# Second stage of a fused attention and mixture-of-experts kernel: norm rows by ScalarE, routing weights from one exponential, slot bases in the rank product, three mixture banks

## The chip, the cores and the metric

One core of a Trainium2 chip runs the whole program. The metric is the device time of one execution in microseconds (us). Three runs of the kernel before gave 1202.75, 1204.52 and 1208.31 us, so the median is 1204.52 us. Engines are named as in the profile: PE is TensorE, DVE is VectorE, ACT is ScalarE, POOL is GpSimd, and SP issues most of the DMAs. PEld is PE's weight load.

## The reference

`x` is 32 samples of 112 rows by 256, and `ctx` is 32 samples of 375 rows by 256. Four residual layers follow one another:

```python
x = x + xattn0(ctx, layernorm(x))         # 16 heads; queries from x, keys and values from ctx
x = x + ffn0(layernorm(x))                # 8 experts relu(x W_e + b_e), mixed by the counts of all top-2 choices
x = x + xattn1(layernorm(x), ctx, ctx, mask)   # softmax(q k^T / 16 + mask * -1e9) v
x = x + ffn1(layernorm(x))                # 8 experts of 256-512-256, each token goes to its top 2

# ffn1
w, idx = top_k(xt @ Wg.T + bg, 2)
w = softmax(w, axis=1)
comb = (one_hot(idx, 8) * w[..., None]).sum(axis=1)
out = einsum('eto,te->to', y, comb)
```

The layer norm divides `x - mean` by `sqrt(var + 1e-5)`. The weight of each of the two experts of a token in `ffn1` is a softmax over its two largest logits.

## The kernel before

The program has three stages. The first does `xattn0` and counts the choices of `ffn0`. It leaves `x_res` (the rows after `xattn0`) and `xT_hi`, `xT_lo` (their norm rows, transposed, as two float16 parts). The third stage runs the experts of `ffn1` over rows that were sorted by expert in DRAM (`dispatch`). The change is in the second stage, `middle_phase`, which spans 585 to 949 us of the profile. Its order of work is written out by hand and unrolled. It has 39 steps. Step `u` does five things on five samples, each where it exists:

- `f`, steps 0 to 31: `ffn0`'s mixture for groups of four samples (`GT` = 448 rows). A step does four mixtures, `mix(0)` to `mix(3)`. In each, PE multiplies six 128x128 by 128x448 float16 products into a PSUM bank (L1035), and DVE adds the clipped result to `acc` (L1199 for the first expert, L1203 for the others). Mixture `k` writes bank `k % 2`, so PE waits before it until DVE has read the mixture two places back (`acc_rdy`).
- `a`, sample `u-4`: PE transposes `acc` back into bank 2 (L1051) and DVE adds it to `x_res` (L1231). DVE takes mean and variance (L1212, L1215). POOL makes `rstd` of the variance (L965, L967). DVE makes the norm rows `x2n` (L1245). PE transposes them (L1075), ACT copies them out (`x2nT`, L1159), and PE makes the scores with `ctxT` in bank 4 (L1095). ACT and POOL also split a piece of `ffn1`'s weights into float16 parts (`w_hi` L1155, `w_lo` L994).
- `o`, sample `u-5`: DVE adds the mask and takes the row maximum (L1223), ACT takes the exponential (L1134), PE transposes it into bank 5 (L1061), ACT copies it out (`probsT`, L1139), PE multiplies with `ctx_rows` (L1069), and DVE adds the result to the residual, which gives `x3` (L1291; the profile calls this tile `we`, whose memory it uses).
- `r`, sample `u-6`: DVE takes the statistics of `x3` (L1212, L1215 again), POOL makes `rstd` and `ln_shift` = -mean * rstd (L981), ACT writes the norm rows into `rows` (L1149), PE transposes them (L1082), ACT and DVE make `xT_hi` and `xT_lo` of them (L1163, L1298), and PE makes the routing logits in bank 7 (L1106).
- `k`, sample `u-7`: DVE adds the bias to the logits, finds the two largest and their places, and makes the one-hot rows `first` and `second` and their sum `chosen` (L1250 to L1267). The softmax of two numbers is made of `gap` = second minus largest logit: ACT takes its exponential (L1142), and DVE makes `gap_sum`, `unscaled` and `first_w` (L1274, L1281, L1284). PE ranks the tokens of each expert in bank 3 (L1088 within the sample, L1089 by the running counts `cum`). DVE adds the expert's first slot (`slot_base`), picks the two slots of each token and rounds them to integers (`slots_at`, L1306 to L1314). POOL scatters `rows` to the two slots with two indirect DMAs (L1011).

Each engine works its own list in order, and semaphores join the lists. POOL's list is of importance here. In a step it stands: the two scatters of the step before, `rstd` of `a` (L965, L967), `rstd` and `ln_shift` of `r`, `mask_add` (L987), `w_lo` (L994), the token numbers (L1001), then the scatters of this step, which wait for `slots_at`.

Of the kernel before, what the change touches and what calls it, by code (L numbers as in the profile page):

```python
# [742 lines left out]
def middle_phase(nc, ctx, dram, keep):  # L743
# [143 lines left out]
    with nc.Block() as block:  # L887

        @block.sync
        def _(sp):  # L890
# [60 lines left out]
        def _(pool):  # L951
# [17 lines left out]
            def step(t, u, on):  # L969
                f, a, o, r, k = on  # L970
                if a:
                    rstd("ag2", "eps2", "rs2", 0, cnt(t, u - LAG_ATT, 1, 1))
                if r:
# [45 lines left out]
        def _(pe):  # L1019
            pe.wait_ge(m["consts"], 3)  # L1020

            nc.tensor.matmul(psum[:, 0, 0:E], ones[:], gate_counts[:], start=True, stop=True).then_inc(m["share_ps"], 1)
            pe.wait_ge(m["share_rdy"], 1)

            def mixture(t, u, k):
# [5 lines left out]
                wait(pe, m["acc_rdy"], cnt(t, u, 4, k - 1))  # L1031
                n = 0
                for w, x in ((we_hi, xT_hi), (we_hi, xT_lo), (we_lo, xT_hi)):
                    for kc in range(DC):
# [4 lines left out]

            def step(t, u, on):  # L1040
# [43 lines left out]
                if k:  # L1084
# [609 lines left out]
```

## Time and profile before

| | us |
|---|---|
| median of three runs | 1204.52 |
| the profiled execution | 1202.87 |
| its span in the profile | 1201.1 |
| PE busy (share of the span) | 998.3 (83%) |
| DVE busy | 812.5 (68%) |
| ACT busy | 533.8 (44%) |
| POOL busy | 437.8 (36%) |

The table is a sum over three stages with different limits. What matters for the change is a stretch of the second stage in which all five parts run, 646.70 to 892.79 us, and the four steps behind it, which have no mixtures. "Idle before, releaser" in a row is how long the engine stood idle before that instruction and what it then had waited for. Of the engine PE the rows show the granted clock as a share of 2.4 GHz. Matmuls are pipelined, so rows of a group overlap, and the starts of rows tell more than their ends.

### The profile page before, as it was taken

The numbers are of one execution on the slowest core, as the hardware profiler recorded it, in microseconds if no ns is written. First come the engines' busy times: TensorE is split into PE (matmuls) and PEld (weight loads), VectorE is DVE, ScalarE is ACT, GpSimd is POOL, SyncE is SP. The second block draws the span as 40 slices with busy tenths as digits, with TensorE's granted clock in tenths as the row PEclk, the third lists the DMA queues.
The fourth block names the chain that finished last, engine by engine and source line by source line (L and its number), as shares of the span: only waits on it lengthen the run. The fifth ranks groups of instructions, "written<-read, shape, count | busy, mean of one in ns | idle before, by whom it ended". The sixth has DMA issues, their size and how long they took to land. (4 is left out here: it accounts for less than half of the span.)

```text
span 1201.1 us, 30730 instructions
## 1 busy us (share of the span) xinstructions
PE 998.3 (83%) x10536; PEld 706.0 (59%) x10536; DVE 812.5 (68%) x2319; ACT 533.8 (44%) x1055; POOL 437.8 (36%) x616
## 2 busy tenths in 40 slices
PE   3688889888888988876499999999986289999993
PEld 2366666666666666654255555555554168888872
DVE  4567777777777777764468888888887436666652
ACT  1365666565566666544113232233333045555551
POOL 4322222222222222200115555555556335555444
PEclk9999999999999999988599999999998579999997
DMA  4543333333333343210445555555554135555443
GB/s 126 148 123 117 105 114 112 110 107 114 118 104 117 101 120 105 86 38 2 128 133 166 151 150 150 152 153 150 151 156 133 50 106 89 101 92 94 86 63 36
DMA packets 104712, 133.93 MB, mean 112 GB/s; under 512 B 23806, under 2 KB 93902, under 8 KB 104398
## 3 DMA queue, kind: packets, MB, share of 16 engines
q1 hardware_dynamic: 91024, 113.86, 32.5%
q0 software_dynamic: 13536, 18.10, 8.8%
q8 instruction: 88, 1.44, 0.5%
q14 instruction: 64, 0.52, 0.2%
HBM read 93.78 MB, written 38.68 MB: 110 GB/s over the span
## 5 line engine op out<-in xcount | busy, mean ns | idle before, releaser
L612 DVE TENSOR_REDUCE smax<-psum 112x2 f32<-112x750 f32 x256 | 235.9, 933 | 120.6 <-PE psum L355 120.6
L526 ACT ACTIVATE probsT<-psum 125x896 f32<-125x896 f32 x192 | 175.9, 916 | 39.2 <-PE psum L370 39.2
L1454 POOL DMA_INDIRECT out_dram<-y,token_at x70 | 109.9, 1570 | 117.1 <-DMA out_dram<-y,token_at 61.0
L1535 ACT ACTIVATE h<-psum,b 128x256 f32<-128x256 f32 x140 | 58.8, 471 | 102.5 <-PE psum L1482 102.5
L296 POOL TENSOR_TENSOR ctx_lo<-ctxT,ctx_hi 128x750 f16<-128x750 f32 x32 | 51.7, 1614 | 133.1 <-ACT ctx_hi L533 133.1
L1011 POOL DMA_INDIRECT dispatch_dram<-rows,slots_at x64 | 64.0, 1000 | 94.1 <-DVE slots_at L1314 78.3
L1035 PE MATMUL psum<-xT_hi,we_hi 128*128 128x448 f16 x256 | 71.2, 360 | 26.2 <-DVE acc L1203 12.8
L390 PE MATMUL psum<-probsT,v_aug 125*32 125x112 f32 x3072 | 90.2, 267 | 0.0
L355 PE MATMUL psum<-k_stack,q_stack 63*128 63x375 f16 x512 | 84.9, 329 | 2.1 <-ACT xnT L566 1.3
L1203 DVE SCALAR_TENSOR_TENSOR acc<-psum,neg_bias,acc 128x448 f32<-128x448 f32 x112 | 75.7, 677 | 8.6 <-PE psum L1035 8.6
L370 PE MATMUL psum<-q_stack,k_stack 64*128 64x112 f16 x1536 | 70.3, 210 | 8.2 <-ACT probsT L526 6.8
L390 PEld LDWEIGHTS psum<-probsT,v_aug 125*32 125x32 f32 x3072 | 74.1, 112 | 5.0
L288 POOL TENSOR_SCALAR ln_var<-ln_mv 112x1 f32<-112x1 f32 x32 | 7.1, 222 | 190.2 <-DVE ln_mv L624 190.2
L1035 PE MATMUL psum<-xT_hi,we_lo 128*128 128x448 f16 x256 | 71.0, 360 | 0.0
L1035 PE MATMUL psum<-xT_lo,we_hi 128*128 128x448 f16 x256 | 70.6, 358 | 0.0
L370 PEld LDWEIGHTS psum<-q_stack,k_stack 64*128 64x128 f16 x1536 | 50.9, 95 | 33.5 <-ACT probsT L526 19.2
L1482 PE MATMUL psum<-x_hi,w_hi 128*128 128x256 f16 x280 | 56.1, 281 | 9.7 <-DVE x_lo L1549 5.8
L1134 ACT ACTIVATE probs<-probs,exp_bias 112x375 f32<-112x375 f32 x32 | 19.4, 607 | 100.0 <-DVE exp_bias L1226 100.0
L1482 PE MATMUL psum<-x_hi,w_lo 128*128 128x256 f16 x280 | 55.2, 280 | 0.0
L1482 PE MATMUL psum<-x_lo,w_hi 128*128 128x256 f16 x280 | 55.0, 279 | 0.0
L1549 DVE TENSOR_TENSOR x_lo<-psum,x_hi 128x512 f16<-128x512 f32 x35 | 24.1, 689 | 43.3 <-ACT x_hi L1526 43.3
L1069 PE MATMUL psum<-ctx_rows,probsT 125*112 125x256 f32 x192 | 49.8, 397 | 2.9 <-issue 2.9
(215 smaller groups left out, 2405.1 us busy)
## 6 DMA issues: line engine op xcount, KB each, us to landing
ctxT<-in_ctxT_dram SPq DMA_DIRECT2D x64, 375.0 KB, 4.2
k_stack<-k_hi_dram SPq DMA_DIRECT2D x64, 188.0 KB, 2.7
ctx_rows<-in_ctx_dram SPq DMA_DIRECT2D x32, 375.0 KB
rows_e<-dispatch_dram SPq DMA_DIRECT2D x70, 136.0 KB, 2.5
w_raw<-in_w_dram SPq DMA_DIRECT2D x32, 256.0 KB, 4.6
k_hi_dram<-k_hi SPq DMA_DIRECT2D x32, 188.0 KB, 1.9
k_lo_dram<-k_lo SPq DMA_DIRECT2D x32, 188.0 KB, 1.9
k_stack<-k_lo_dram SPq DMA_DIRECT2D x32, 188.0 KB, 2.8
```

Source lines behind the costliest of these rows:

```text
L296: nc.gpsimd.tensor_tensor(ctx_lo[:, u % 2, :, :], ctxT[:, u % 2, :, :], ctx_hi[:, u % 2, :, :], ALU.subtract).then_inc(m["ctxlo_ready"], 1)
L355: last = nc.tensor.matmul(psum[:, pair_bank(s) + a, 0:KV], queries(rows, b4, s, 128), keys_at(rows, b4, s, 0, KV), start=True, stop=True)
L370: last = nc.tensor.matmul(psum[:, a, r * S:(r + 1) * S], keys_at(rows, b4, 4 * hg + r, c * KC, 128), queries(rows, b4, 4 * hg + r, S), sta ...
L390: last = nc.tensor.matmul(bank_d[32 * j:32 * j + 32, g * S:(g + 1) * S], v_aug[:, b4d, cc, h, :], probsT[:, b2d, cc, h // 8, h % 2, h // 2 ...
L526: nc.scalar.activation(probsT[:, p, c, hg, :, :, :].rearrange("p k h q -> p k (h q)"), psum[0:KC, 0:2, 0:4 * S], ACT.Exp, scale=float(HD) ...
L612: nc.vector.reduce_max(smax[:, (u - LAG_B) % 2, 2 * (s % 4) + s // 4::PAIRS], psum[0:S, pair_bank(s):pair_bank(s) + 2, 0:KV], AX.X).then_i ...
L1011: nc.gpsimd.indirect_dma_start(dram["dispatch"], bass.IndirectOffsetOnAxis(slots_at[:, uk % ROW_SLOTS, n:n + 1], 0), rows[:, uk % ROW_SLOT ...
L1035: last = nc.tensor.matmul(psum[:, k % 2, 0:GT], w[:, kc, e, hc * 128:(hc + 1) * 128], x[:, kc, bass.ds(g0, GT)], start=(n == 0), stop=(n = ...
L1203: nc.vector.scalar_tensor_tensor(out, psum[:, k % 2, 0:GT], neg_bias[:, hc, e:e + 1], out, ALU.max, ALU.add).then_inc(m["acc_rdy"], 1)
L1454: nc.gpsimd.indirect_dma_start(dram["out"], bass.IndirectOffsetOnAxis(token_at[:, n % 2, s:s + 1], 0), y[:, n % 2, s, :], None, compute_op ...
L1482: last = nc.tensor.matmul(psum[:, 1 + c // 2, (c % 2) * TILE:(c % 2 + 1) * TILE], w[:, bass.ds(e, 1), kc, c * 128:(c + 1) * 128].rearrange ...
L1535: nc.scalar.activation(h[:, c, :], psum[:, 1 + c // 2, (c % 2) * TILE:(c % 2 + 1) * TILE], ACT.Relu, bias=b1[:, c, bass.ds(e, 1)]).then_in ...
```

## The change

It has five parts, all in the second stage.

1. `x2n` moves from DVE to ACT. POOL makes a second `ln_shift` (`shift2`), right behind `rstd` of `a`, and ACT computes `x * rstd + shift` behind `probsT`.
2. The routing weights come from `exp(logits - largest)` of all eight logits, by one ACT instruction. One DVE instruction multiplies them with `chosen` and sums them (`weight_sum`), and its reciprocal is `first_w`. `gap`, `gap_sum` and the `unscaled` of before go.
3. The slot bases are a 113th row of `cum` (and `ones` gets a 113th row), so the second rank product adds them. `slot_of` goes.
4. Two DVE instructions that multiply and sum pick the two slots straight from PSUM, in place of two products and a reduction.
5. The rank product moves from bank 3 to bank 5, behind the transposed exponentials, with two waits for it on PE. Mixtures take banks 0, 1 and 3 in turn, and PE waits for the mixture three places back.

```diff
 # POOL, first in a step
                 if a:
-                    rstd("ag2", "eps2", "rs2", 0, cnt(t, u - LAG_ATT, 1, 1))
+                    v = cnt(t, u - LAG_ATT, 1, 1)
+                    rstd("ag2", "eps2", "rs2", 0, v)
+                    wait(pool, m["rs2"], v)
+                    wait(pool, m["x2n_rdy"], cnt(t, u - LAG_ATT - 1, 1, 1))
+                    apart(pool)
+                    nc.gpsimd.tensor_scalar(ln_shift[:, 0, :], ln_mv[:, 0, 0:1], ln_rstd[:, 0, :], -1.0, ALU.mult, ALU.mult).then_inc(m["shift2"], 1)
...
 # PE
+        return MIX_BANKS[(4 * (t * TURN + u) + k) % len(MIX_BANKS)]      # (0, 1, 3)
-                wait(pe, m["acc_rdy"], cnt(t, u, 4, k - 1))
+                wait(pe, m["acc_rdy"], cnt(t, u, 4, k + 1 - len(MIX_BANKS)))
-                        last = nc.tensor.matmul(psum[:, k % 2, 0:GT], ...
+                        last = nc.tensor.matmul(psum[:, mix_bank(t, u, k), 0:GT], ...
...
                     wait(pe, m["exp_rdy"], cnt(t, uo, 1, 1))
                     wait(pe, m["pT_rdy"], cnt(t, uo - 1, 1, 1))
+                    wait(pe, m["pick_rdy"], cnt(t, uk - 1, 2, 2))
...
                     wait(pe, m["chosen_rdy"], cnt(t, uk, 1, 1))
                     wait(pe, m["cum_rdy"], cnt(t, uk - 1, 1, 1))
-                    nc.tensor.matmul(psum[0:S, 3, 0:E], before[:], chosen[:], start=True, stop=False)
-                    nc.tensor.matmul(psum[0:S, 3, 0:E], ones[:, 0:S], cum[:], start=False, stop=True).then_inc(m["rank_done"], 1)
+                    if o:
+                        wait(pe, m["pT_rdy"], cnt(t, uo, 1, 1))
+                    if isinstance(t, int) and t * TURN + uk == 0:
+                        pe.wait_ge(m["weights_in"], 16 * N_W)
+                    rank = psum[0:S, RANK_BANK, RANK_AT:RANK_AT + E]
+                    nc.tensor.matmul(rank, before[:], chosen[:], start=True, stop=False)
+                    nc.tensor.matmul(rank, ones[:, 0:S], cum[:], start=False, stop=True).then_inc(m["rank_done"], 1)
...
 # ACT
+                if a:
+                    xrow = x_res[:, bass.ds(t * TURN + ua, 1), :].rearrange("p o d -> p (o d)")
+                    wait(act, m["shift2"], cnt(t, ua, 1, 1))
+                    apart(act)
+                    wait(act, m["x2nT_done"], cnt(t, ua - 1, 1, 1))
+                    nc.scalar.activation(x2n[:], xrow, ACT.Identity, bias=ln_shift[:, 0, :], scale=ln_rstd[:, 0, :]).then_inc(m["x2n_rdy"], 1)
                 if k:
-                    wait(act, m["gap_rdy"], cnt(t, uk, 1, 1))
-                    nc.scalar.activation(gap_exp[:], gap[:], ACT.Exp).then_inc(m["gexp_rdy"], 1)
+                    wait(act, m["negtop_rdy"], cnt(t, uk, 1, 1))
+                    wait(act, m["pair_rdy"], cnt(t, uk - 1, 1, 1))
+                    nc.scalar.activation(logit_exp[:], logits[:], ACT.Exp, bias=neg_top[:]).then_inc(m["lexp_rdy"], 1)
...
 # DVE
-                if a:
-                    v = cnt(t, ua, 1, 1)
-                    wait(dve, m["rs2"], v)
-                    wait(dve, m["x2nT_done"], cnt(t, ua - 1, 1, 1))
-                    nc.vector.tensor_scalar(x2n[:], xrow(ua), ln_mv[:, 0, 0:1], ln_rstd[:, 0, :], ALU.subtract, ALU.mult).then_inc(m["x2n_rdy"], 1)
...
-                    nc.vector.tensor_tensor(gap[:], top8[:, 1:2], top8[:, 0:1], ALU.subtract).then_inc(m["gap_rdy"], 1)
+                    nc.vector.tensor_scalar(neg_top[:], top8[:, 0:1], -1.0, None, ALU.mult).then_inc(m["negtop_rdy"], 1)
...
-                    wait(dve, m["gexp_rdy"], v)
-                    nc.vector.tensor_scalar(gap_sum[:], gap_exp[:], 1.0, None, ALU.add).then_inc(m["pair_rdy"], 1)
+                    wait(dve, m["lexp_rdy"], v)
+                    wait(dve, m["chosen_rdy"], v)
+                    nc.vector.tensor_tensor_reduce(out=unscaled[:], in0=logit_exp[:], in1=chosen[:], scale=1.0, scalar=0.0,
+                                                   op0=ALU.mult, op1=ALU.add, accum_out=weight_sum[:]).then_inc(m["pair_rdy"], 1)
...
-                    nc.vector.scalar_tensor_tensor(unscaled[:], second[:], gap_exp[:], first[:], ALU.mult, ALU.add).then_inc(m["pair_rdy"], 1)
...
-                    nc.vector.tensor_tensor(slot_of[:], psum[0:S, 3, 0:E], slot_base[:], ALU.add).then_inc(m["pos_rdy"], 1)
-                    nc.vector.tensor_tensor(cum[:], cum[:], chosen[:], ALU.add).then_inc(m["cum_rdy"], 1)
-                    wait(dve, m["pos_rdy"], v)
-                    nc.vector.tensor_tensor(picked[:, 0, :], slot_of[:], first[:], ALU.mult).then_inc(m["pick_rdy"], 1)
-                    nc.vector.tensor_tensor(picked[:, 1, :], slot_of[:], second[:], ALU.mult).then_inc(m["pick_rdy"], 1)
-                    wait(dve, m["pick_rdy"], cnt(t, uk, 3, 2))
-                    nc.vector.tensor_reduce(slots[:], picked[:], AX.X, ALU.add).then_inc(m["pick_rdy"], 1)
+                    for n, which in enumerate((first, second)):
+                        nc.vector.tensor_tensor_reduce(out=picked[:, n, :], in0=psum[0:S, RANK_BANK, RANK_AT:RANK_AT + E], in1=which[:], scale=1.0,
+                                                       scalar=0.0, op0=ALU.mult, op1=ALU.add, accum_out=slots[:, n:n + 1]).then_inc(m["pick_rdy"], 1)
+                    nc.vector.tensor_tensor(cum[0:S, :], cum[0:S, :], chosen[:], ALU.add).then_inc(m["cum_rdy"], 1)
```

The instructions of DVE in the middle of a full step, before, from the statistics of `x3` to the second mixture:

```order
L1212 BN_STATS ln_stats<-we 112x6 [waits m_x3_rdy]
L1215 BN_AGGR ln_mv<-ln_stats 112x2 [waits m_st3]
L1245 TENSOR_SCALAR x2n<-x_res,ln_mv,ln_rstd 112x256 [waits m_x2nT_done,m_rs2]
L1250 TENSOR_TENSOR logits<-psum,route_bias 112x8 [waits m_route_done]
L1253 MAX top<-logits 112x8 [waits m_lg_rdy]
L1256 TENSOR_TENSOR gap<-top 112x1 [waits m_gexp_rdy,m_top_rdy]
L1258 MAX_INDEX top_at<-top,logits 112x8
L1203 SCALAR_TENSOR_TENSOR acc<-psum,neg_bias,acc 128x448 [waits m_acc_rdy,m_ffn_done]
```

The same place on DVE now:

```order
L1234 BN_STATS ln_stats<-we 112x6 [waits m_x3_rdy]
L1237 BN_AGGR ln_mv<-ln_stats 112x2 [waits m_st3]
L1268 TENSOR_TENSOR logits<-psum,route_bias 112x8 [waits m_lexp_rdy,m_route_done]
L1271 MAX top<-logits 112x8 [waits m_lg_rdy]
L1273 TENSOR_SCALAR neg_top<-top 112x1 [waits m_top_rdy]
L1275 MAX_INDEX top_at<-top,logits 112x8
L1225 SCALAR_TENSOR_TENSOR acc<-psum,neg_bias,acc 128x448 [waits m_acc_rdy,m_ffn_done]
```

DVE no longer has `x2n` here, nor its wait for POOL's `rs2`.

The end of a full step on DVE, before, from the third mixture to the integer slots:

```order
L1203 SCALAR_TENSOR_TENSOR acc<-psum,neg_bias,acc 128x448 [waits m_acc_rdy,m_ffn_done]
L1298 TENSOR_TENSOR xT_lo<-psum,xT_hi 128x2x112 [waits m_x3hi_rdy]
L1303 TENSOR_SCALAR rows<-unscaled,first_w 112x8 [waits m_pair_rdy]
L1306 TENSOR_TENSOR slot_of<-psum,slot_base 112x8 [waits m_rank_done]
L1307 TENSOR_TENSOR cum<-cum,chosen 112x8
L1309 TENSOR_TENSOR picked<-slot_of,first 112x8 [waits m_pos_rdy]
L1310 TENSOR_TENSOR picked<-slot_of,second 112x8
L1312 TENSOR_REDUCE slots<-picked 112x2 [waits m_pick_rdy]
L1314 CAST slots_at<-slots 112x2 [waits m_pick_rdy]
```

The same place on DVE now (an ISA row is one multiply-and-sum; the row of one column behind it reads its sum out):

```order
L1225 SCALAR_TENSOR_TENSOR acc<-psum,neg_bias,acc 128x448 [waits m_acc_rdy,m_ffn_done]
L1315 TENSOR_TENSOR xT_lo<-psum,xT_hi 128x2x112 [waits m_x3hi_rdy]
L1320 TENSOR_SCALAR rows<-unscaled,first_w 112x8 [waits m_sumw_rdy]
L1324 ISA picked,slots<-psum,first 112x8 [waits m_rank_done]
L1324 ISA slots 112x1
L1324 ISA picked,slots<-psum,second 112x8
L1324 ISA slots 112x1
L1326 TENSOR_TENSOR cum<-cum,chosen 112x8
L1328 CAST slots_at<-slots 112x2 [waits m_pick_rdy]
```

The five small instructions between `rows` and `slots_at` became five others, with one wait among them fewer.

ACT in a full step, before:

```order
L1134 ACTIVATE probs,prob_sum<-probs,exp_bias 112x375 [waits m_eb_rdy]
L1139 ACTIVATE probsT<-psum 125x336 [waits m_o_done,m_pT_done]
L1142 ACTIVATE gap_exp<-gap 112x1 [waits m_gap_rdy]
L1149 ACTIVATE rows<-we,ln_shift,ln_rstd 112x256 [waits m_scattered0,m_rows_set,m_shift3]
L1155 ACTIVATE w_hi<-w_raw 128x512 [waits m_w_in0]
L1159 ACTIVATE x2nT<-psum 128x224 [waits m_s1_done,m_x2nT_done]
L1163 ACTIVATE xT_hi<-psum 128x2x112 [waits m_x3nT_done]
```

ACT in a full step now:

```order
L1149 ACTIVATE probs,prob_sum<-probs,exp_bias 112x375 [waits m_eb_rdy]
L1154 ACTIVATE probsT<-psum 125x336 [waits m_o_done,m_pT_done]
L1160 ACTIVATE x2n<-x_res,ln_shift,ln_rstd 112x256 [waits m_shift2,m_x2nT_done]
L1164 ACTIVATE logit_exp<-logits,neg_top 112x8 [waits m_pair_rdy,m_negtop_rdy]
L1171 ACTIVATE rows<-we,ln_shift,ln_rstd 112x256 [waits m_scattered0,m_rows_set,m_shift3]
L1177 ACTIVATE w_hi<-w_raw 128x512 [waits m_w_in0]
L1181 ACTIVATE x2nT<-psum 128x224 [waits m_s1_done,m_x2nT_done]
L1185 ACTIVATE xT_hi<-psum 128x2x112 [waits m_x3nT_done]
```

`x2n` stands between `probsT` and the exponential of the logits.

## Rows read from the trace of the kernel before

**Rows 1.** Busy time by stretch (share of span in us, instructions), PEclk, DMA share, GB/s.
```profile
646.70:892.79 246.09, 222.74 (x1271) 137.50 (x1269) 206.35 (x816) 73.75 (x192) 137.72 (x240) 1.00 0.52 153
892.79:928.37 35.58, 25.56 (x114) 16.81 (x114) 25.40 (x120) 11.92 (x32) 22.99 (x40) 0.81 0.49 143
```
**Rows 2.** Waits of the second stage: who waited for whom, us, times, longest.
```profile
DVE x2n L1245 <- POOL ln_rstd L967: 23.7, 30, 1.4
...
PE psum L1035 <- DVE acc L1203: 12.8, 35, 0.7
```
**Rows 3.** DVE in one full step: start us, us, instruction [idle before <-releaser].
```profile
728.85 0.17 DVE L1314 CAST slots_at<-slots 112x2 uint32<-112x2 f32 x1
729.10 0.55 DVE L1223 CUSTOM_DVE_ANT_0 probs<-psum,mask_add 112x375 f32<-112x375 f32 x1
...
732.23 0.18 DVE L1215 BATCH_NORM_AGGREGATE ln_mv<-ln_stats 112x2 f32<-112x6 f32 x1
733.15 0.41 DVE L1245 TENSOR_SCALAR x2n<-x_res,ln_mv,ln_rstd 112x256 f32<-112x256 f32 x1 [0.74 <-POOL ln_rstd L967]
733.48 0.16 DVE L1250 TENSOR_TENSOR logits<-psum,route_bias 112x8 f32<-112x8 f32 x1
...
736.12 0.89 DVE L1281 SCALAR_TENSOR_TENSOR unscaled<-second,gap_exp,first 112x8 f32<-112x8 f32 x1
...
737.39 0.67 DVE L1203 SCALAR_TENSOR_TENSOR acc<-psum,neg_bias,acc 128x448 f32<-128x448 f32 x1
...
739.08 0.17 DVE L1314 CAST slots_at<-slots 112x2 uint32<-112x2 f32 x1
```
**Rows 4.** POOL in the same step.
```profile
729.88 1.05 POOL L1011 DMA_INDIRECT dispatch_dram<-rows,slots_at  x1 [2.82 <-DVE slots_at L1314]
...
732.22 0.25 POOL L965 TENSOR_SCALAR ln_var<-ln_mv 112x1 f32<-112x1 f32 x1
732.55 0.57 POOL L967 TENSOR_TENSOR ln_rstd<-ln_var,half 112x1 f32<-112x1 f32 x1
...
734.23 0.27 POOL L981 TENSOR_SCALAR ln_shift<-ln_mv,ln_rstd 112x1 f32<-112x1 f32 x1 [0.24 <-POOL ln_rstd L967]
...
735.83 1.15 POOL L994 TENSOR_TENSOR w_lo<-w_raw,w_hi 128x512 f16<-128x512 f32 x1 [0.85 <-ACT w_hi L1155]
```
**Rows 5.** ACT in the same step.
```profile
734.53 0.60 ACT L1149 ACTIVATE rows<-we,ln_shift,ln_rstd 112x256 f32<-112x256 f32 x1
735.04 0.61 ACT L1155 ACTIVATE w_hi<-w_raw 128x512 f16<-128x512 f32 x1
735.56 0.34 ACT L1159 ACTIVATE x2nT<-psum 128x224 f32<-128x224 f32 x1
```
**Rows 6.** PE in the same step.
```profile
734.25 0.36 PE L1075 MATMUL psum<-ident,x2n 112*128 112x112 f32 x2
735.05 0.55 PE L1035 MATMUL psum<-xT_hi,we_hi 128*128 128x448 f16 x2 [0.44 <-DVE acc L1199]
...
736.20 0.36 PE L1082 MATMUL psum<-ident,rows 112*128 112x112 f32 x2
...
736.72 1.50 PE L1095 MATMUL psum<-ctxT,x2nT 128*112 128x375 f32 x4
```
**Rows 7.** Single lines over the whole run: duration ns min/median/max, first and last start.
```profile
L1281 DVE SCALAR_TENSOR_TENSOR unscaled<-second,gap_exp,first x32: 205/949/1031, 643.3 to 944.7; 112x8 f32<-112x8 f32 x32
```
**Rows 8.** The same view of L1223, and its sum's read-out.
```profile
L1223 DVE CUSTOM_DVE_ANT_0 probs<-psum,mask_add x32: 548/549/550, 620.7 to 928.4; 112x375 f32<-112x375 f32 x32
L1223 DVE DVE_READ_ACCUMULATOR2_ANT row_max<- x32: 82/84/85, 621.2 to 928.8; 112x1 f32 x32
```
**Rows 9.** PE at the start of the stage.
```profile
594.08 0.54 PE L1035 MATMUL psum<-xT_hi,we_hi 128*128 128x448 f16 x2 [3.01 <-DVE acc L1199]
```
**Rows 10.** DVE in the first step without mixtures, which begins at 892.79.
```profile
900.17 0.53 DVE L1303 TENSOR_SCALAR rows<-unscaled,first_w 112x8 f32<-112x8 f32 x1
...
901.54 0.55 DVE L1223 CUSTOM_DVE_ANT_0 probs<-psum,mask_add 112x375 f32<-112x375 f32 x1
```

More of the change, by code:

```diff
@@ L836, in middle_phase @@
     top8_at = sb("top8_at2", [S, 8], U32)
-    gap = sb("gap", [S, 1], F32)
-    gap_exp = sb("gap_exp", [S, 1], F32)
-    gap_sum = sb("gap_sum", [S, 1], F32)
+    neg_top = sb("neg_top", [S, 1], F32)
+    logit_exp = sb("logit_exp", [S, E], F32)
+    weight_sum = sb("weight_sum", [S, 1], F32)
     first_w = sb("first_w", [S, 1], F32)
@@ L845, in middle_phase @@
         ffn_done accT_done x2nT_done s1_done pT_done o_done x3nT_done route_done
-        x2nT_rdy exp_rdy pT_rdy x3hi_rdy gexp_rdy
+        x2nT_rdy exp_rdy pT_rdy x3hi_rdy lexp_rdy
         acc_rdy x2_rdy st2 ag2 x2n_rdy masked_rdy eb_rdy inv_rdy x3_rdy st3 ag3 x3n_rdy x3lo_rdy
-        lg_rdy top_rdy at_rdy gap_rdy pair_rdy which_rdy comb_rdy chosen_rdy rank_done pos_rdy pick_rdy slots_rdy
+        lg_rdy top_rdy at_rdy negtop_rdy pair_rdy sumw_rdy which_rdy comb_rdy chosen_rdy rank_done pick_rdy slots_rdy
         cum_rdy token_rdy scattered0 scattered1 scattered2 scattered3 x3_out0 x3_out1 pads_out w_in0 w_in1 w_hi_rdy w_lo_rdy rows_set late_in tally_done table
-        eps2 rs2 eps3 rs3 shift3 mask_rdy""".split()
+        eps2 rs2 eps3 rs3 shift2 shift3 mask_rdy""".split()
     m = {n: sem("m_" + n) for n in names}
@@ L1020, in _ @@
             pe.wait_ge(m["consts"], 3)
-            nc.tensor.matmul(psum[:, 0, 0:E], ones[:], gate_counts[:], start=True, stop=True).then_inc(m["share_ps"], 1)
+            nc.tensor.matmul(psum[:, 0, 0:E], ones[0:S, :], gate_counts[:], start=True, stop=True).then_inc(m["share_ps"], 1)
             pe.wait_ge(m["share_rdy"], 1)
@@ L1112, in _ @@
             pe.wait_ge(m["cum_rdy"], B)
-            nc.tensor.matmul(psum[:, 0, 0:E], ones[:], cum[:], start=True, stop=True).then_inc(m["tally_done"], 1)
+            nc.tensor.matmul(psum[:, 0, 0:E], ones[0:S, :], cum[0:S, :], start=True, stop=True).then_inc(m["tally_done"], 1)
             pe.wait_ge(m["table"], TABLE_OPS)
@@ L1148, in step @@
                     wait(act, m["shift3"], cnt(t, ur, 1, 1))
-                    nc.scalar.activation(rows[:, ur % ROW_SLOTS, 0:D], x3[:, ur % 2, :], ACT.Identity, bias=ln_shift[:],
+                    nc.scalar.activation(rows[:, ur % ROW_SLOTS, 0:D], x3[:, ur % 2, :], ACT.Identity, bias=ln_shift[:, 1, :],
                                          scale=ln_rstd[:, 1, :]).then_inc(m["x3n_rdy"], 1)
@@ L1249, in step @@
                     wait(dve, m["route_done"], v)
+                    wait(dve, m["lexp_rdy"], cnt(t, uk - 1, 1, 1))
                     nc.vector.tensor_tensor(logits[:], psum[0:S, 7, DC * S:DC * S + E], route_bias[:], ALU.add).then_inc(m["lg_rdy"], 1)
@@ L1280, in step @@
                 if k:
-                    nc.vector.scalar_tensor_tensor(unscaled[:], second[:], gap_exp[:], first[:], ALU.mult, ALU.add).then_inc(m["pair_rdy"], 1)
-                if k:
-                    wait(dve, m["pair_rdy"], cnt(t, uk, 3, 1))
-                    nc.vector.reciprocal(first_w[:], gap_sum[:]).then_inc(m["pair_rdy"], 1)
+                    wait(dve, m["pair_rdy"], cnt(t, uk, 1, 1))
+                    nc.vector.reciprocal(first_w[:], weight_sum[:]).then_inc(m["sumw_rdy"], 1)
                 if o:
```

28 lines of the change are left out of this document (14 added, 14 removed).

## Prediction

> **What bounds the kernel now.** I read first the busy time by stretch, to find where the change lies. From 646.70 to 892.79 us the second stage does 24 full steps, 10.25 us each. PE works 222.74 us of it, 9.28 per step, at a granted clock of 1.00 [rows 1]. So PE is near its limit there but idles 0.97 us per step. DVE is busy 206.35 us, 8.6 per step. Neither is the bound by its busy share, so I looked at the waits: the longest of DVE's is for POOL's rstd, 30 times and 23.7 us in all, and PE's is for DVE, to have a mixture read out of its bank [rows 2].
>
> One step in order of time then shows the loop that sets the 10.25. Let T be the end of `slots_at`, 728.85 + 0.17 = 729.02 [rows 3]. POOL starts the first scatter 0.86 later, goes on to ln_var at T+3.20, and ends rstd at 733.12, T+4.10 [rows 4]. DVE's statistics were done at 732.41, yet `x2n` starts at 733.15, when rstd is there. From the start of `x2n` to the end of the next `slots_at` (739.25) DVE takes 6.10 us with no other wait of note [rows 3]. 4.10 + 0.03 + 6.10 = 10.23. So the loop is: slots, two scatters and rstd on POOL, `x2n`, the rest of DVE's list, slots. PE is beside it: it stands idle 0.44 us before the fourth mixture because DVE's second one came late [rows 6].
>
> **The change, part by part.** I compare three sums per full step: PE's work, DVE's list, and what is left of the loop through POOL.
>
> PE: nothing is taken away. It keeps 9.28 us [rows 1]. The rank product has 113 rows in place of 112, which I cost at nothing, and its two new waits are for things long done: the slots picked in the step before, 2.8 us ahead in PE's list (two mixtures and the transposed `acc`), and `probsT`, which the product with `ctx_rows` has already waited for. The third bank ends PE's wait for a mixture two places back as long as DVE is less than three behind.
>
> DVE: (a) `x2n` and its wait go: 732.41 to 733.48 without them is about 0.08, so -1.0 us [rows 3]. (b) `unscaled` takes 0.949 in the middle, 0.205 at best [rows 7]. It ran 736.12 to 737.01, and POOL's `w_lo` 735.83 to 736.98 [rows 3, 4]: DVE was held until POOL was done. The new multiply-and-sum stands in that place but earlier in time, since DVE gains (a), while `w_lo` comes later (below). Unheld I cost it as `unscaled` at best plus a read-out, 0.205 + 0.084 [rows 7, 8], and gap_sum goes: -0.7. (c) From the start of the fourth mixture to the end of `slots_at` it was 1.86 [rows 3]. The two new multiply-and-sums replace sum, two products and a reduction: about -0.15. The sum is 10.25 - 1.85 = 8.4. The new form is not in the trace at 8 columns. Bounds: from below the 0.205 of `unscaled` without its read-out (it has the same width, so it can hardly be less), from above the 0.549 of the same kind of instruction at 375 columns [rows 8]. I take the row of equal width with the read-out. At the upper end three of them add 1.0 to DVE, 9.4 in all.
>
> POOL loop: shift2 adds what shift3 shows, 0.24 + 0.27 = 0.51 [rows 4], and everything behind it on POOL moves by that. shift3 ended at 734.50, T+5.48, now T+5.99. `rows` on ACT 0.03 later takes 0.60; `w_hi` starts 0.51 after `rows` and takes 0.61, so ends at T+7.14 [rows 5]. `w_lo` follows 0.18 later and takes 1.15: T+8.47 [rows 4]. The DVE instruction that writes the weights into `rows` can be held by it: 0.53 in the tail step of [rows 10], where `w_lo` ran beside it. It then ends near T+8.5, and the slots 0.6 later: 9.1. This loop is under PE's 9.28, but by only 0.2; at the upper end of the new form it is 9.1 + 2 x 0.34 = 9.8.
>
> `x2n` itself: ready at T + 4.61 + 0.03 + 0.60 = T+5.24, with the 0.60 of ACT's `rows` of the same shape [rows 5]. PE reaches its transposes 6.25 after the end of the scores (738.22 less one period, to 734.25), 0.5 of it its own waits, so 5.75 [rows 6]. `slots_at` can then be done 0.1 before the scores' end (the fourth mixture's last product ends some 0.2 behind 736.20; DVE needs 1.7 from there, PE 1.8), so `x2n` has 0.6 us to spare. ACT has the room: 73.75 of 246.09 us busy [rows 1].
>
> On the hold the Trainium skill (SBUF — State Buffer, Who interferes with whom) says that a VectorE instruction with two SBUF inputs contends with a GpSimd instruction that reads SBUF, and that whichever starts first keeps the shared ports for its whole length. By that rule the new multiply-and-sum of the weights, both of whose inputs are in SBUF, can be held as `unscaled` was, while the two on the slots, with one input in PSUM, can't. If it started behind `w_lo`, (b) would be worth nothing; the trace agrees with the rule, 0.949 against 0.205. By my times it starts at T+6.0, ahead of `w_lo` at T+7.3, but close to `mask_add`.
>
> The exponential of 8 logits with a bias I cost at the 0.2 us of ACT's time for one number, off every loop: `probsT` is long done and shift3 comes later. The Trainium skill (ScalarE: Activation LUTs, What ACT_TABLE_LOAD costs) gives 93 ns more for a per-partition bias; by it, too, nothing would end later.
>
> So PE becomes the bound: 9.28, and I take 9.32 for imperfect meetings. 24 x (10.25 - 9.32) = 22.3 us less. Start of the stage: PE idled 3.01 us because DVE read the first mixtures late [rows 9]; with a third bank it does one mixture there, worth 735.05 to 736.20, 1.15 us, at full clock [rows 6]: -1.3 with a little for the low clock. The four steps without mixtures take 35.58 us, 8.9 each [rows 1]. There DVE's savings meet the later `w_hi`: `x2nT` on ACT comes behind it at T+7.4, the scores take 1.5, so T+8.95, against a first such step of 901.54 - 892.79 = 8.75 [rows 10]: 0.2 each, and more where the clock is low (0.81 on average [rows 1]), +1.1 for the four. Sum: -22.3 - 1.3 + 1.1 = -22.5. Against the profiled execution's 1202.87 that is 1180.4. The median of the runs was 1.65 above it; I forecast 1181.5.
>
> **The rivals.**
> - POOL's loop stays the bound. For it: the margin is 0.2 us, all of it small instructions, and the hold by `w_lo` or `mask_add`. Against it: each of its terms has a row. Half way to its upper end it gives 9.6 us per step, 24 x 0.28 = 7 us less gain: 1188.
> - The bound moves and nothing is won: PE's transposes wait for an `x2n` that now comes by POOL, shift2 and ACT. It needs `x2n` 1.6 us later than T+5.24, 0.97 for PE's idle time and the 0.6 that I count to spare; ACT behind a late `probsT` could do part of that. About 1203.
> - The other side, slower: PE as the bound makes the clock the bound. At 1.00 there is no sign of it [rows 1], but the tail has 0.81. At a mean of 0.905 in the full steps, 9.28 becomes 10.25 and the gain is gone; below that the kernel is slower. At 0.88 it is 10.55: 24 x 0.3 + 1 for the tail, 1212.
> - The change does less than it says: the new multiply-and-sum is held by `mask_add` each time (0.5) and is 0.55 long, so DVE needs 9.9: 1195.
>
> **How the numbers follow.** PE as the bound 0.66, 1176 to 1186 by itself. POOL's loop 0.17, 1186 to 1194. Multiply-and-sum dear 0.05, 1195. Nothing won 0.06, 1203. Clock, slower 0.06, 1212. The range runs from 1176, where all of PE's idle time goes (-23.3), the start gives 3 and the tail costs nothing, to 1193, within the second case. What this measurement can tell from no change is about 0.5%, 6 us. Faster has the first three cases, 0.88; within 0.5% 0.06; slower 0.06.
>
> **What would show it.** Right: the starts of the mask-and-maximum (now L1245) 9.3 us apart in full steps; PE's idle time before mixtures near nothing; DVE waiting for PE's scores or fourth mixture instead; PE's granted clock at 1.00. L1292 at 0.2 to 0.3 us. `x2n` on ACT ending before PE's product with `ctx_rows` does. Steps of the tail at 8.9 or a little more. Wrong: PE idle before the transposes of `x2n` with ACT as releaser, L1292 near 1 us, or DVE idle for nothing of PE's while steps are 9.6 or longer.

## The result and the profile after

The changed kernel takes 1171.64 us, the median of 4 runs (1167.92 to 1173.98), against 1206.26 us of the kernel before on the same chips. The ratio is 0.9722, 95% interval 0.9688 to 0.9755. It is faster, as forecast, but by more: 1181.5 was forecast and 1176 was the low end of the range. The profiled execution took 1170.19 us, its span is 1168.2.

The stretches of the second stage in both traces, cut at the same events (the start of the mask-and-maximum of sample 3, of sample 27 and of sample 31), us:

| stretch | before | after | difference | forecast |
|---|---|---|---|---|
| product of the counts to the first mask-and-maximum | 40.05 | 36.00 | -4.05 | -1.3 |
| three steps of filling up | 25.98 | 24.76 | -1.22 | 0 |
| 24 full steps | 246.09 | 215.57 | -30.52 | -22.3 |
| four steps without mixtures | 35.58 | 36.68 | +1.10 | +1.1 |
| everything outside | 853.40 | 855.19 | +1.8 | 0 |

What lies outside is untouched code, but for the last steps of the second stage, up to the last slots, which took 17.22 us against 18.21 before. Its two sides moved against each other here (the second stage began 6.70 us later, the rest behind took 4.91 less), and in the fourteen profiled kernels of this study the part behind the start of the last scatter, which no edit touches, varied from 246.5 to 252.4 us. All comparisons are of fast runs; one of the later runs of the kernel before took 2446.72 us in the slow state and is not used.

The busy time by stretch of the changed kernel, which answers to [rows 1] (span, PE, PEld, DVE, ACT, POOL busy, PEclk, DMA share, GB/s):

```profile
648.13:863.70 215.57, 213.41 (x1274) 139.31 (x1274) 185.86 (x793) 85.29 (x216) 144.70 (x264) 1.00 0.56 175
863.70:900.38 36.68, 26.03 (x117) 16.72 (x116) 21.74 (x116) 14.35 (x36) 24.11 (x44) 0.81 0.48 148
```

A full step takes 8.98 us. The same products of PE that were "222.74 us busy" in [rows 1] are now 213.41 us busy, at the same granted clock (1.00). So the earlier figure held something other than work.

DVE in one full step of the changed kernel, in order of time, which answers to [rows 3]:

```profile
746.65 0.17 DVE L1328 CAST slots_at<-slots 112x2 uint32<-112x2 f32 x1
747.14 0.55 DVE L1245 CUSTOM_DVE_ANT_0 probs<-psum,mask_add 112x375 f32<-112x375 f32 x1 [0.32 <-PE psum L1110]
...
750.20 0.18 DVE L1237 BATCH_NORM_AGGREGATE ln_mv<-ln_stats 112x2 f32<-112x6 f32 x1
750.31 0.17 DVE L1268 TENSOR_TENSOR logits<-psum,route_bias 112x8 f32<-112x8 f32 x1
...
752.76 0.16 DVE L1292 CUSTOM_DVE_ANT_0 unscaled<-logit_exp,chosen 112x8 f32<-112x8 f32 x1
...
753.84 0.68 DVE L1225 SCALAR_TENSOR_TENSOR acc<-psum,neg_bias,acc 128x448 f32<-128x448 f32 x1 [0.22 <-PE psum L1044]
754.57 0.39 DVE L1315 TENSOR_TENSOR xT_lo<-psum,xT_hi 128x224 f16<-128x224 f32 x1
754.88 0.54 DVE L1320 TENSOR_SCALAR rows<-unscaled,first_w 112x8 f32<-112x8 f32 x1
755.33 0.15 DVE L1324 CUSTOM_DVE_ANT_0 picked<-psum,first 112x8 f32<-112x8 f32 x1
...
755.61 0.17 DVE L1328 CAST slots_at<-slots 112x2 uint32<-112x2 f32 x1
```

The logits start 0.11 us after the last row of the statistics, where `x2n` and its wait stood. The multiply-and-sum of the weights takes 0.16 in this step and is not held. DVE now waits for PE, 0.32 before the mask-and-maximum. The row that writes the weights into `rows` takes 0.54 in place of the 0.22 that is its median in the full steps before: it is held. POOL in the same step, which answers to [rows 4]:

```profile
747.69 1.06 POOL L1020 DMA_INDIRECT dispatch_dram<-rows,slots_at  x1 [0.95 <-DVE slots_at L1328]
...
751.17 0.27 POOL L981 TENSOR_SCALAR ln_shift<-ln_mv,ln_rstd 112x1 f32<-112x1 f32 x1 [0.24 <-POOL ln_rstd L971]
...
752.63 0.27 POOL L990 TENSOR_SCALAR ln_shift<-ln_mv,ln_rstd 112x1 f32<-112x1 f32 x1 [0.24 <-POOL ln_rstd L971]
...
754.24 1.16 POOL L1003 TENSOR_TENSOR w_lo<-w_raw,w_hi 128x512 f16<-128x512 f32 x1 [0.85 <-ACT w_hi L1177]
```

`w_lo` ends at 755.40 and the held row at 755.42. From `slots_at` (746.82) to the end of `w_lo` is 8.58 us, and from there to the next `slots_at` (755.78) 0.38: 8.96, the period. So by this reading the loop through POOL, which the prediction had at 9.1 and put second, is the bound. PE's rows alone would not show it, since PE is busy for 99% of the full steps; the experiments below do. The line of the weights over the whole run, min/median/max ns:

```profile
L1292 DVE CUSTOM_DVE_ANT_0 unscaled<-logit_exp,chosen x32: 154/158/501, 645.0 to 916.3; 112x8 f32<-112x8 f32 x32
```

The maximum is a hold too: in 6 of the 24 full steps the instruction took 0.43 to 0.50 us and ended about 0.01 us after POOL's `mask_add`. The prediction's last rival had this hold in each step.

### The profile page after: what moved, and what is told of

Its sections match the earlier page's. It is cut to its first block and busy times, and to the rows that moved or that the text cites. A ratio compares the mean times of both kernels' runs of the same rounds, so it can differ in the third digit from the quotient of the medians.

```text
span 1168.2 us, 30858 instructions
## 1 busy us (share of the span) xinstructions
PE 989.8 (85%) x10536; PEld 710.5 (61%) x10536; DVE 784.8 (67%) x2287; ACT 550.5 (47%) x1087; POOL 448.7 (38%) x648
## 3 DMA queue, kind: packets, MB, share of 16 engines
q1 hardware_dynamic: 90898, 113.86, 32.7%
## 5 line engine op out<-in xcount | busy, mean ns | idle before, releaser
L1496 PE MATMUL psum<-x_lo,w_hi 128*128 128x256 f16 x280 | 54.1, 275 | 0.0
L545 ACT ACTIVATE k_hi<-psum 128x375 f16<-128x375 f32 x64 | 31.1, 487 | 46.1 <-PE psum L406 46.1
```

The source lines that it names most:

```text
L1496: last = nc.tensor.matmul(psum[:, 1 + c // 2, (c % 2) * TILE:(c % 2 + 1) * TILE], w[:, bass.ds(e, 1), kc, c * 128:(c + 1) * 128].rearrange ...
```

## The experiments

Theory A: the full steps of the changed kernel are set by the loop slots, scatters, rstd, two shifts, `rows`, `w_hi`, `w_lo`, held row, slots; PE's own list needs only about 8.75 us, and the 9.28 of the prediction was PE's busy time with waits hidden in it. Rival C is the prediction's view, that PE's list is the bound. Results are in one table. "Full step" is the mean of the 24 full steps in the profile. The ratio, with its 95% interval, is to runs of the kernel before that were made beside each group: their medians were 1206.26 us for the changed kernel, 1206.68 for u1 to u4, 1205.65 for the p runs and v1, and 1201.17 for b1, b2, v3 and v6. So ratios can be compared across groups, medians only roughly.

| kernel | median us | ratio | full step us |
|---|---|---|---|
| before | | | 10.254 |
| changed | 1171.64 | 0.9722 (0.9688 to 0.9755) | 8.982 |
| u1, two banks | 1170.70 | 0.9723 (0.9646 to 0.9800) | 8.965 |
| u2, `x2n` on DVE | 1194.73 | 0.9916 (0.9887 to 0.9945) | 10.068 |
| u3, weights of the gap | 1168.02 | 0.9700 (0.9643 to 0.9758) | 8.965 |
| u4, three operations pick | 1174.59 | 0.9748 (0.9670 to 0.9825) | 9.181 |
| p1, one more product | 1172.11 | 0.9724 (0.9661 to 0.9787) | 8.983 |
| p4, four more products | 1182.75 | 0.9813 (0.9745 to 0.9881) | 9.490 |
| pb, before, one more product | 1207.67 | 1.0012 (0.9980 to 1.0044) | 10.256 |
| v1, scatters a step later | 1157.06 | 0.9608 (0.9531 to 0.9685) | 8.734 |
| b1, before, `x2n` on ACT | 1184.94 | 0.9875 (0.9831 to 0.9919) | 9.416 |
| b2, before, scatters later | 1187.49 | 0.9876 (0.9833 to 0.9919) | 9.703 |
| v3, weight row last | 1164.54 | 0.9708 (0.9662 to 0.9753) | 8.783 |
| v6, v1 and v3 | 1161.56 | 0.9667 (0.9626 to 0.9707) | 8.734 |

The untouched parts vary by several us between executions, so the full step is the sharper number: within one trace 19 or more of the 24 steps lie within 0.02 us of their median (14 in b1 and b2). The totals missed their stated ranges in nine runs, by 0.1 us in v3, 0.5 in p1, pb and b2, 1.3 in u1, 1.6 in v6, 2.6 in u3, 2.9 in p4 and 3.1 in u4; only u2, v1 and b1 met them. The readings below rest on the full steps.

**Parts undone, one at a time.** u1:

```diff
-    MIX_BANKS = (0, 1, 3)
+    MIX_BANKS = (0, 1)
```

> The changed kernel with mixtures in banks 0 and 1 alone, as before. Theory A (the full steps, 8.97 us each, are set by the loop through POOL: slots, scatters, rstd, shift2, shift3, rows, w_hi, w_lo, the held weight row, slots; PE's list alone needs about 8.75): in full steps DVE has read the bank two places back in time everywhere, so the period stays 8.97 +- 0.05; only the start of the stage loses 1 to 4 us. Total 1172 to 1176. Rival B (the third bank is what freed PE in the full steps): PE idles before mixtures again, period 9.3 or more, total 1180 or more.

The full step is unchanged, 8.965, so the third bank is worth nothing there. The start of the stage took 38.11 us against 36.00, which agrees with a worth of 1 to 4 us but does not measure it (see the term of the start below). u2 puts the DVE instruction of `x2n` back between the statistics and the logits, waiting for `rs2`, and takes shift2 and ACT's instruction out:

```diff
-                    nc.gpsimd.tensor_scalar(ln_shift[:, 0, :], ln_mv[:, 0, 0:1], ln_rstd[:, 0, :], -1.0, ALU.mult, ALU.mult)
-                    nc.scalar.activation(x2n[:], xrow, ACT.Identity, bias=ln_shift[:, 0, :], scale=ln_rstd[:, 0, :])
+                    nc.vector.tensor_scalar(x2n[:], xrow(ua), ln_mv[:, 0, 0:1], ln_rstd[:, 0, :], ALU.subtract, ALU.mult)
```

> The changed kernel with the norm rows x2n made by DVE again, behind POOL's rstd, and without shift2. Theory A: the old loop is back, slots, scatters, rstd, x2n, DVE's list, slots, shorter than before only by the cheaper pick (0.4 us): period 9.7 to 9.9, total 1189 to 1195. Rival (the gain lies in the routing arithmetic and the banks): period under 9.3, total under 1180.

10.07: the long step is back, and longer than theory A's 9.7 to 9.9. The trace shows where the saving of the cheaper pick was lost. One step of u2, DVE and below it POOL:

```profile
704.52 0.41 DVE L1257 TENSOR_SCALAR x2n<-x_res,ln_mv,ln_rstd 112x256 f32<-112x256 f32 x1 [0.80 <-POOL ln_rstd L971]
...
707.29 1.08 DVE L1287 CUSTOM_DVE_ANT_0 unscaled<-logit_exp,chosen 112x8 f32<-112x8 f32 x1
```

```profile
707.20 1.15 POOL L999 TENSOR_TENSOR w_lo<-w_raw,w_hi 128x512 f16<-128x512 f32 x1 [0.86 <-ACT w_hi L1167]
```

The same instruction that takes 0.16 in the changed kernel takes 1.08 here, to the end of `w_lo`. I had given the cheaper pick as saved and forgotten that the new weight instruction, started 0.09 behind `w_lo`, is held for all of it. So moving `x2n` does two things: it ends the wait for rstd, and it brings the weights ahead of `w_lo`.

The second is what the period shows. These are medians over the full steps, us, of the period cut at the end of `w_lo`:

| kernel | slots to the end of `w_lo` | from there to the next slots | sum |
|---|---|---|---|
| before | 7.97 | 2.26 | 10.23 |
| u2 | 7.97 | 2.12 | 10.09 |
| b1 | 8.64 | 0.78 | 9.42 |
| u4 | 8.60 | 0.57 | 9.17 |
| changed | 8.57 | 0.39 | 8.96 |

In the kernel before, `unscaled` started at slots + 7.04 and ended at 7.99, 0.02 behind `w_lo`, in each of the full steps. Unheld it would have ended at 7.25, by its shortest time of 0.205, so by this estimate DVE had 0.74 us to spare between `x2n` and that point, and POOL's list up to `w_lo`, with the DVE row that it held, closed the loop. ACT's `rows`, from which `w_hi` and `w_lo` follow, started 0.03 us after shift3 in both kernels. But the exponential of the gap, which stands in front of it on ACT and comes later by DVE's wait for rstd, had ended only 0.14 us earlier, so the two paths were close. The change made POOL's part 0.60 longer and took 1.87 from what stands behind it. u3 makes the weights of the gap again:

```diff
-                    nc.vector.tensor_tensor_reduce(out=unscaled[:], in0=logit_exp[:], in1=chosen[:], ..., accum_out=weight_sum[:])
+                    nc.vector.tensor_scalar(weight_sum[:], logit_exp[:, 0:1], 1.0, None, ALU.add)
+                    nc.vector.scalar_tensor_tensor(unscaled[:], second[:], logit_exp[:, 0:1], first[:], ALU.mult, ALU.add)
```

(here `logit_exp[:, 0:1]` holds the exponential of the gap.)

> The changed kernel with the routing weights made of the exponential of the gap, as before (one DVE instruction more, unscaled with two SBUF inputs). Theory A: unscaled now starts near slots + 6.0, ahead of w_lo, so it is not held and takes about 0.2 us; DVE has room there (it waits for PE before the fourth mixture), period unchanged at 8.97, total within 1 us of the changed kernel. Rival: it is held by w_lo as before, 0.9 us, period 9.3 or more, total +8 or more.

Unchanged, 8.965. Part 2 of the change is worth nothing by itself. The expectation that `unscaled` would not be held was wrong, though: in 21 of the 24 full steps it took 0.34 to 0.49 us, held by `mask_add` and not by `w_lo`, and the step had room for it:

```profile
710.64 0.52 POOL L996 TENSOR_SCALAR mask_add<-mask 112x375 f32<-112x375 f32 x1
710.70 0.48 DVE L1298 SCALAR_TENSOR_TENSOR unscaled<-second,logit_exp,first 112x8 f32<-112x8 f32 x1
```

u4:

```diff
-                        nc.vector.tensor_tensor_reduce(out=picked[:, n, :], in0=psum[...], in1=which[:], ..., accum_out=slots[:, n:n + 1])
+                        nc.vector.tensor_tensor(picked[:, n, :], psum[...], which[:], ALU.mult)
+                    nc.vector.tensor_reduce(slots[:], picked[:], AX.X, ALU.add)
```

> The changed kernel with the slots picked by two products and one reduction in place of two multiply-and-sums (the slot bases stay in the rank product). Theory A: these stand behind the row that w_lo holds, on the loop itself, so their whole extra length, 0.2 to 0.35 us per step, lengthens the period: 9.15 to 9.3, total +6 to +9 us. Rival C (PE is the bound, as was forecast): DVE has 0.3 us to spare before the scores come, period unchanged, total +0 to 1.

9.18, +0.20 per step: instructions between the held row and `slots_at` are on the loop. DVE idled 0.32 us a little later in the changed kernel, and that idle time did not cover them. In the medians the 5 us of 24 steps are lost in the scatter (+3).

**PE's own list, measured by a dose.** p1 and p4 repeat a product in the fourth, or in each, mixture of a step; pb does it in the kernel before:

```diff
+                for _ in range(1 if k in (3,) else 0):      # p4: (0, 1, 2, 3)
+                    nc.tensor.matmul(psum[:, bank, 0:GT], we_hi[:, 0, e, hc * 128:(hc + 1) * 128], xT_hi[:, 0, bass.ds(g0, GT)], start=True, stop=True)
```

> The changed kernel with one 128x128 by 128x448 float16 product repeated in the fourth mixture of each step (0.19 us of PE's list at full clock; the result is the same). Theory A (POOL's loop sets the full steps, PE has about 0.2 us to spare): full steps stay at 8.97 to 9.03, total +1 to +2 us. Rival C (PE is the bound): +0.19 per step in all 32 steps with mixtures, +6 us.

> The same with one product repeated in each of the four mixtures (0.76 us of PE's list per step). Theory A: PE becomes the bound, 8.75 + 0.76 = 9.5 us per full step, which measures PE's own list; total +14 to +19. Rival C: 8.97 + 0.76 = 9.73 per full step, total +24.

> The kernel before with one product repeated in the fourth mixture of each step. My theory: PE's list had 1.4 us to spare per full step there, more than its idle time shows, and the fourth mixture is off the loop through rstd and x2n: period stays at 10.25, total +0 to +1.5 us. Rival (PE was beside the bound with the end of the fourth mixture on the loop): +0.19 per step, +6 us.

One product more is free in both kernels (8.983, 10.256). Four more give 9.490: 4 x 0.19 = 0.76 on a list of 8.73. PE is busy without a gap in the full steps of p4, of v1 (below) and also of p1, in this order:

```profile
645.07:872.84 227.77, 227.77 (x1370) 149.89 (x1370) 179.83 (x792) 87.89 (x216) 144.68 (x264) 1.00 0.55 165
```

```profile
644.91:854.53 209.62, 209.62 (x1274) 140.55 (x1274) 177.32 (x792) 87.89 (x216) 143.78 (x263) 1.00 0.59 178
```

```profile
643.51:859.09 215.58, 215.56 (x1299) 142.96 (x1298) 183.67 (x793) 85.99 (x216) 144.69 (x264) 1.00 0.58 175
```

So a PE without a gap does not prove that PE is the bound: in p1 it had taken in a further product at no cost. What tells is the dose, and how even the steps are. In p4 and v1 all 24 agree within 0.01 us; in p1 they run from 8.82 to 9.27, as in the changed kernel.

**The loop, cut in two places.** v1 issues a sample's scatters one step later, at the same place of POOL's list:

```diff
-                if k:
-                    uk = u - LAG_SEND
-                    ... waits and two scatters of uk ...
+                if k and t * TURN + (u - LAG_SEND) > 0:
+                    send(t, u - LAG_SEND - 1)
...
+            send(B // TURN, -1)
```

> The changed kernel with the two scatters of a sample issued one step later, at the same place in POOL's list, so that POOL waits for slots that are long there, and rstd no longer stands behind this step's slots. Theory A: the loop is cut; full steps fall to PE's own list, 8.7 to 8.8 us, and the steps without mixtures fall by more, 1 to 3 us each; total -7 to -16 us against the changed kernel, 1156 to 1165. Rival C: PE is the bound, full steps stay at 8.97, only the tail gains, total -4 to -8.

8.734 in every full step, PE's own list. The whole falls to 1157.06 us (ratio 0.9608). Of the 13.6 us between its profiled span and that of the changed kernel, 24 x 0.248 = 6.0 are the full steps, and 3.8 lie before and behind the second stage, in code that the edit does not touch. One expectation failed, that the steps without mixtures fall by 1 to 3 us each. The four in the table above took 36.56, 0.1 less than in the changed kernel, and the last steps, up to the last slots, 14.13, which is 3.1 less. PE's clock in the four differs between traces, and at nearly the same mean granted clock the late scatters show there too: 36.56 (v1, 0.72) against 38.46 (u1, 0.73), and 32.96 (v6, below, 0.90) against 36.30 (u3, 0.91). So they are worth some 3 us or more in all steps without mixtures together, with one trace each. v3 leaves the scatters and moves the held row from before the picks to behind `slots_at` (only the added lines are shown):

```diff
                     wait(dve, m["pick_rdy"], cnt(t, uk, 2, 2))
                     nc.vector.tensor_copy(slots_at[:, uk % ROW_SLOTS, :], slots[:]).then_inc(m["slots_rdy"], 1)
+                    wait(dve, m["sumw_rdy"], v)
+                    nc.vector.tensor_scalar(rows[:, uk % ROW_SLOTS, AT_W:AT_W + E], unscaled[:], first_w[:], None, ALU.mult)
```

> The changed kernel with the DVE row that writes the routing weights moved behind slots_at, so that the slots no longer stand behind a row that w_lo holds. Theory A: that hold is part of the loop of 8.97 us; without it the loop is shorter than PE's list, and full steps fall to PE's own 8.73. Total -5 to -7 us against the changed kernel. Rival (POOL's own chain up to w_lo and the scatters is the loop, the hold is beside it): full steps stay at 8.9 to 8.97.

8.78: moving one instruction of 0.22 us behind `slots_at` takes 0.20 off each step. In a step of it the row, its neighbours and POOL's `w_lo` are:

```profile
746.50 1.16 POOL L1003 TENSOR_TENSOR w_lo<-w_raw,w_hi 128x512 f16<-128x512 f32 x1 [0.85 <-ACT w_hi L1177]
```

```profile
747.21 0.15 DVE L1321 CUSTOM_DVE_ANT_0 picked<-psum,first 112x8 f32<-112x8 f32 x1
...
747.38 0.30 DVE L1323 TENSOR_TENSOR cum<-cum,chosen 112x8 f32<-112x8 f32 x1
747.60 0.16 DVE L1325 CAST slots_at<-slots 112x2 uint32<-112x2 f32 x1
747.67 0.22 DVE L1327 TENSOR_SCALAR rows<-unscaled,first_w 112x8 f32<-112x8 f32 x1
```

The picks, with one input in PSUM, run beside `w_lo` at 0.15 to 0.16 us. `cum`, with two in SBUF, is held to its end in the weight row's stead (0.30 at the median against 0.18 in the changed kernel), so v3 stays 0.05 above PE's own list.

> Late scatters and the weight row last together, on the changed kernel. Both theories: full steps are PE's own list with either edit, so 8.73 again and no more; total as with the late scatters alone, 1155 to 1160. If PE's list could still be shortened by waits that neither edit touches, it would show here as less than 8.73.

8.734 again, so nothing is left in the full steps but PE's products. The total is above the range that was expected; the intervals of v6 and v1 overlap.

**One part alone, on the kernel before.** b1 adds shift2 and ACT's `x2n` and takes DVE's out, with banks, weights and slots as before; b2 makes v1's edit there.

> The kernel before with one part of the change alone: x2n made by ACT behind POOL's second shift. Theory A: DVE no longer waits for rstd and comes to unscaled ahead of w_lo, so that is no longer held; the loop through POOL and w_lo is left, and the old slot arithmetic stands behind the held row, 0.4 us longer than the new one. Full steps 9.3 to 9.45 us, total 1182 to 1187, two thirds or more of the whole gain. Rival (the gain needs the cheaper routing or the banks): full steps 9.8 or more, total 1194 or more.

> The kernel before with its two scatters issued one step later, nothing else. Theory A: the loop slots, scatters, rstd, x2n is cut; DVE's list becomes the bound, with unscaled still held by w_lo. Full steps 9.55 to 9.7 us, total 1188 to 1193. Rival (the wait for rstd is not set by the scatters): full steps stay above 10.1, total 1202 or more.

b1 gives 9.416, so it takes off 0.84 of the 1.27 us that the whole change took off a full step, and the ratio is 0.9875. The trace has `unscaled` at 0.21 us and the slots behind the held row as theory A has it:

```profile
743.90 0.21 DVE L1287 SCALAR_TENSOR_TENSOR unscaled<-second,gap_exp,first 112x8 f32<-112x8 f32 x1
...
746.23 0.53 DVE L1309 TENSOR_SCALAR rows<-unscaled,first_w 112x8 f32<-112x8 f32 x1
...
747.35 0.17 DVE L1320 CAST slots_at<-slots 112x2 uint32<-112x2 f32 x1
```

b2 gives 9.703, the upper end of the 9.55 to 9.7: DVE's wait for rstd is gone and `unscaled` is still held, 1.03 at the median and in 23 of 24 steps. POOL now waits for DVE's statistics (`ln_var`, 54.1 us in the full steps) and DVE for nearly nothing, which fits DVE's list, with the hold in it, as the bound.

## Why the prediction was wrong

The direction and most of what each edit does on DVE were right. The time was outside the range mainly because of one term, PE's own list.

- **The step that failed** is "PE: nothing is taken away. It keeps 9.28 us". 9.28 was PE's busy time in [rows 1] over 24. PE's own list takes 8.734 (v1, v6, and 9.490 less the dose of 0.76 in p4). The busy time of a matmul reaches to its modelled end, and where the next instruction has to wait, the tail of the last one, which otherwise lies beside the next, counts as busy. In [rows 6] the scores start at 736.72 and the products behind them, which waited for `xT_lo`, at 738.41 (0.19 idle shown), so 1.69; in v1, without a wait, the two starts are 704.34 and 705.67, 1.33. The wait cost 0.36, of which the idle column shows half. The other 0.17 is how far the scores' 1.50 reach beyond the next start in v1. Over the step PE had 10.25 - 8.73 = 1.52 us of waits where I read 0.97. The rows, before and then v1:

```profile
738.41 0.27 PE L1106 MATMUL psum<-route_whi,xT_hi 128*112 128x8 f16 x2 [0.19 <-DVE xT_lo L1298]
```

```profile
704.34 1.50 PE L1112 MATMUL psum<-ctxT,x2nT 128*112 128x375 f32 x4
705.67 0.22 PE L1123 MATMUL psum<-route_whi,xT_hi 128*112 128x8 f16 x2
```

- **What is the bound.** "PE becomes the bound" was wrong: POOL's loop is, as the first rival had it, though not at 9.6 but at 8.96. My own sum for it was 9.1; `w_lo` ended at slots + 8.58 in place of 8.47, and the slots followed in 0.38 in place of 0.6, since the new multiply-and-sum takes 0.15 at 8 columns, less than the 0.205 + 0.084 that I took, and overlaps its read-out. Had I trusted no floor from busy time, my own sum of the POOL loop would have given 9.1 and 24 x 1.15 = 27.6, about 1176.7 in all by the other terms: nearer, and at the low end of the range.
- **The loop before was read wrong at one link.** I had it as slots, scatters, rstd, `x2n`, the rest of DVE's list, 4.10 + 0.03 + 6.10. Those 6.10 us hold DVE's stand behind `w_lo`, which I had seen and priced as a saving on DVE, not as part of the loop. The table under u2 shows it: the period is POOL's 7.97 to the end of `w_lo` and 2.26 behind it. The gain came as forecast from moving `x2n`, by the second of its two effects more than by the end of the wait, and how much the first would give alone is not separated.
- **Term of 24 full steps:** forecast 22.3, measured 30.5. This 8.2 is four fifths of the error of the forecast against the two profiled executions (22.5 against 32.7). The forecast's last step also has a slip of 0.5: 1180.4 + 1.65 is 1182.0, not 1181.5.
- **Term of the start:** forecast 1.3, measured 4.05. I had one bank's worth in it and nothing for the clock. Without added products the kernels with three banks took 35.19 to 36.50 us here, those with two 36.48 (b1), 37.43 (b2), 38.11 (u1) and 40.05 (before). So the third bank's worth lies between nothing and some 2 us, and these traces don't pin it down. The granted clock over the start was 0.82 before and 0.86 after. `x2n` of the first sample, which took 1.73 us beside POOL's `w_lo` before, has no part in it: u2 has it on DVE, 1.73 long as well, and took 36.01 against 36.00. The three steps of filling up give another 1.2, for which I had no term.
- **Term of the tail:** forecast +1.1, measured +1.10. The size is luck: four such steps varied from 32.96 (v6) to 39.27 us (b1) among these kernels, with mean granted clocks of 0.90 and 0.72, and the single steps do not show the 0.2 each that I gave them (8.75, 10.19, 7.89, 8.75 before; 10.49, 8.32, 8.90, 8.98 after).
- **Right:** the weights ahead of `w_lo` and not held by it; the weight row held; the granted clock at 1.00. `x2n` on ACT was in time, but with far less than the 0.6 us to spare: it ended at 752.15, slots + 5.33 against my 5.24, and PE's transposes started at 752.31, since PE's list is shorter than I took it. Over the full steps PE's weight load waited for it 14 times, 2.6 us in all:

```profile
PEld psum L1085 <- ACT x2n L1160: 2.6, 14, 0.4
```

- **What hid in the sum:** part 2 of the change is worth 0 (u3), the third bank 0 in full steps (u1), the two multiply-and-sums of part 4 0.20 us per step (u4), part 1 most of it (b1 from one side, u2 from the other: 1.09).

On the hold, the Trainium skill (SBUF — State Buffer, Who interferes with whom) says that a VectorE instruction with two SBUF inputs contends with a GpSimd instruction that reads SBUF. The traces agree with it in both directions: the same multiply-and-sum of two SBUF tiles took 0.158 us at the median in the changed kernel, where `w_lo` comes later, and 1.080 in u2, where it ran beside `w_lo`; its like with one input in PSUM took 0.15 beside `w_lo` (v3). The weight row, a `tensor_scalar` on SBUF tiles, shows a hold as well, 0.535 at the median in the changed kernel against 0.22 where `w_lo` had ended (v3).

## What to carry to other kernels

Don't take an engine's busy time as the least time of its list when the engine waits in between: read starts of neighbours in a place where nothing waits, or add a known dose of work and see what the period does. When a loop sets the pace, go round it instruction by instruction, the held ones too: an instruction that is held by another engine puts that engine's list into the loop. A 0.22 us instruction moved out of the loop was worth 0.20 us per step, as much as the cheaper pick of part 4. The loop itself could be cut by issuing the scatters a step later, which gave 0.25 us per full step and some 3 us at the end of the stage beyond the change, about 0.8% of the time. The ratios (0.9608 in v1, 0.9667 in v6, against 0.9722) hold differences of untouched parts as well.

## What the runs showed that I had not expected

- The multiply-and-sum of 8 columns takes 0.154 us, and its read-out of 0.08 lies mostly beside the next instruction. The mask-and-maximum of 375 columns takes 0.549.
- POOL starts its first scatter 0.87 us after `slots_at` at the median of the full steps in each kernel in which it waits for them. In v3, where the slots were done before POOL came, the scatter started 0.75 us after the instruction in front of it, with nothing shown as waited for, and in the shown step of v1, where the slots were a step old, 0.15 us after.
- The exponential of 8 logits with a bias took 0.286 us against 0.20 for one number without. It cost nothing in the full steps, where no row of DVE waited for it.
